# Macaron stage: order of VectorE's work in a step, form of five small VectorE operations, and where GpSimd adds and scales

## The reference

```python
def attn_layer(x, Wqkv, qs, ksc, Wo):              # x is shift_tokens(x), 16 heads of 64
    q, k, v = split(x @ Wqkv)
    q = l2norm(q) * qs;  k = l2norm(k) * ksc       # one length per token and head
    q = q * cos * scale + rotate_half(q) * sin * scale
    k = k * cos * inv + rotate_half(k) * sin * inv
    ...                                            # windows of 32: this one and the one before, softmax, times v
    return out @ Wo
def ffn_layer(x, g, bln, W1, b1, W2, b2):          # x is shift_tokens(x)
    xn = (x - mean) / sqrt(var + 1e-05) * g + bln
    a, gate = split(xn @ W1 + b1)
    return a * gelu(gate) @ W2 + b2
```

## Time and profile before

| | |
|---|---|
| median of 3 runs | 4523.4 us (4511.47 to 4524.17) |
| the profiled execution | 4541.07 us, span 4539.3 us |
| busy share of the span | PE 89%, VectorE 74%, GpSimd 60%, ScalarE 58% |
| macaron stages | 50 to about 1847 us and 1942 to about 3741 us of the span, with the linear attention between them |
| chain that ended last | PE 66%, VectorE 17%, issue 8%, ScalarE 4%, GpSimd 4% |

### The profile page before, as it was taken

One profiled execution on the slowest core, in us unless ns is written; L12 is line 12 of the kernel. 1 busy time (PEld: TensorE's weight loads), 2 busy tenths in 40 slices (PEclk: granted clock), 3 DMA queues, 4 the chain that ended last, 5 costly groups with the idle time before them and its releaser, 6 DMA issues.

```text
span 4539.3 us, 161990 instructions
## 1 busy us (share of the span) xinstructions
PE 4035.5 (89%) x70897; PEld 2573.9 (57%) x70897; DVE 3337.3 (74%) x5613; ACT 2635.8 (58%) x4548; POOL 2704.3 (60%) x3554
## 2 busy tenths in 40 slices
PE   4999999999999999479999999999999985899975
PEld 2666666666666666346666666666666653333333
DVE  5887788878877877478778888788777754667744
ACT  3666666666666665046666666666666641356651
POOL 4777777777777776277777777777777760100000
PEclk9999999999999999789999999999999997689996
DMA  2000000000000000000000000000000000000000
GB/s 81 5 4 24 9 8 20 9 23 7 7 23 9 23 5 9 20 3 9 4 24 10 24 4 9 23 10 23 4 9 5 5 4 0 1 1 1 1 1 9
DMA packets 75299, 53.51 MB, mean 12 GB/s; under 512 B 48472, under 2 KB 71400, under 8 KB 72944
## 3 DMA queue, kind: packets, MB, share of 16 engines
q1 hardware_dynamic: 74608, 43.28, 3.4%
HBM read 35.93 MB, written 1.05 MB: 8 GB/s over the span
## 4 chain that ended last, share of the span: by engine, by line
PE 66%; DVE 17%; issue 8%; ACT 4%; POOL 4%; DVEq 1%; SPq 0%; POOLq 0%; DMA 0%; ACTq 0%
PE psum L343 8%; PE psum L354 8%; PE psum L365 7%; PE psum L427 7%; DVE turn L631 6%; PE psum L390 5%; PE psum L408 5%; PE psum L419 3%; DVE den L676 3%; PE psum L1148 3%; PE psum L490 3%; PE psum L507 3%; PE psum L1117 2%; PE psum L497 2%; PE psum L1136 2%
## 5 line engine op out<-in xcount | busy, mean ns | idle before, releaser
L631 DVE TENSOR_TENSOR turn<-psum,ropes 128x512 f32<-128x512 f32 x1536 | 937.4, 671 | 23.7 <-POOL qkr L734 19.0
L741 POOL TENSOR_TENSOR turn<-turn 128x1024 f32<-128x1024 f32 x384 | 904.1, 2377 | 7.9 <-DVE turn L631 7.9
L343 PE MATMUL psum<-wqkv,xT 128*128 128x512 f32 x1536 | 769.0, 624 | 43.4 <-DVE turn L631 41.2
L526 ACT ACTIVATE sq<-psum 128x512 f32<-128x512 f32 x768 | 456.0, 594 | 578.0 <-PE psum L343 577.9
L734 POOL TENSOR_TENSOR qkr<-turn,rn 128x1024 f32<-128x1024 f32 x384 | 753.3, 1983 | 15.1
L768 POOL TENSOR_TENSOR scratch<-scratch,rden 128x1024 f32<-128x1024 f32 x192 | 365.7, 1905 | 658.0 <-DVE rden L679 658.0
L408 PEld LDWEIGHTS psum<-scratch,V 32*64 32x64 f32 x29952 | 547.3, 132 | 182.7 <-issue 181.4
L408 PE MATMUL psum<-scratch,V 32*64 32x64 f32 (+1 forms) x29952 | 592.7, 222 | 6.7 <-issue 4.6
L354 PE MATMUL psum<-wqkv,xT 128*64 128x512 f32 x1536 | 435.1, 646 | 124.1 <-DVE turn L631 124.1
L365 PEld LDWEIGHTS psum<-ident,qkr 128*128 128x128 f32 x3072 | 340.7, 145 | 353.4 <-ACT kT L535 154.3
L365 PE MATMUL psum<-ident,qkr 128*128 128x128 f32 x3072 | 479.8, 291 | 11.8 <-POOL qkr L734 11.8
(11 more groups left out here) (181 smaller groups left out, 6362.7 us busy)
## 6 DMA issues: line engine op xcount, KB each, us to landing
wqkv<-in_L_ffn_Wqkv_dram SPq DMA_DIRECT2D x12, 1536.0 KB, 7.2
wo<-in_L_ffn_Wo_dram SPq DMA_DIRECT2D x12, 512.0 KB, 7.5
zs<-Y SPq DMA_DIRECT2D x192, 31.8 KB
w<-in_L_ffn_W_dram SPq DMA_DIRECT2D x12, 341.0 KB
zs<-Y SPq DMA_DIRECT2D x168, 0.2 KB
w<-in_L_ffn_W_dram SPq DMA_DIRECT2D x12, 128.0 KB
rope<-in_shape_consts_dram SPq DMA_DIRECT2D x1, 1024.0 KB
X<-in_L_attn_x_dram SPq DMA_DIRECT2D x2, 512.0 KB
```

The source lines that it names most:

```text
L343: pe.matmul(bank[b][:, :], xT[:, n // TPB % 2, bass.ts(n % TPB, P)], wqkv[n // TILES % 2][:, INNER * w:INNER * w + INNER].rearrange("p (h ...
L526: act.activation(sq[:, q // 2, q % 2, :, :], bank[QK_BANK[q]][:, :].rearrange("p (h d) -> p h d", d=RH), ACT.Square).then_inc(sem("squared ...
L631: e = dve.tensor_tensor(dst, src, tab.unsqueeze(1).broadcast_to([P, HEADS, RH]), ALU.mult)
L741: pool.tensor_tensor(t1, t1, turn2[:, w, :, :, :].rearrange("p a h d -> p (a h d)"), ALU.add).then_inc(sem("added"), 1)
```

## The change

Five things move or change form.

VectorE's order in a step: `rotate(u, 0)` and `rotate(u, 1)` follow the subtraction of the maximum, ahead of the softmax sum; the statistics of v and the norm of z come after `rotate(u, 3)`; the aggregation of the statistics stands between the two `lengths`. The two norm operations become `scalar_tensor_tensor` with the inverse root broadcast from `rn` as a tensor in SBUF; the addition of epsilon and the floor become `tensor_tensor` with constant tiles `eps` and `least` in SBUF. GpSimd's `add` writes its sum into `qkr`, in the order that the transposes read, and for that waits until the last transposes of the tile before have read `qkr`; `scale` multiplies `qkr` in place. `rotate(u, 0)` and `rotate(u, 2)` wait for the `add` of the tile before, where they waited for its `scale`. The shifted tile `zs` has three buffers where it had two. The attention over V used two PSUM banks before as after; the diff has nothing on it.

```diff
-        zs = sb("zs", [P, 2, HALF])
+        zs = sb("zs", [P, 3, HALF])
+        least = sb("least", [P, 32])
...
-            if n >= 2:
-                sp.wait_ge(sem("unit_normed"), at.part(n - 2, "unit_normed"))
+            if n >= 3:
+                sp.wait_ge(sem("unit_normed"), at.part(n - 3, "unit_normed"))
...
                 if on(n - 1) and a == 0:
-                    dve.wait_ge(sem("qk_rotated"), part(n - 1, "qk_rotated", w))
+                    dve.wait_ge(sem("added"), part(n - 1, "added", w))
...
-                if on(z):
-                    dve.wait_ge(sem("rnorm"), at.step(s - 1))
-                    if on(z - 1):
-                        dve.wait_ge(sem("mixed"), mixed(s - 1))
-                    dve.tensor_scalar(zn[:, 0:HALF], Y[:, z % TILES, 0:HALF], mv[:, 0:1], rn[:, 32:33], ALU.subtract,
-                                      ALU.mult)
-                    dve.tensor_scalar(zn[:, HALF:D], zs[:, z % 2, :], mv[:, 0:1], rn[:, 32:33], ALU.subtract,
-                                      ALU.mult).then_inc(sem("unit_normed"), 1)
-                if on(v):
-                    dve.wait_ge(sem("shifted%d" % (v % 2)), at.shifted(v))
-                    dve.bn_stats(st6[:, 0, :], Y[:, v % TILES, 0:HALF])
-                    dve.bn_stats(st6[:, 1, :], zs[:, v % 2, :]).then_inc(sem("unit_stats"), 1)
                 if on(u):
                     rotate(u, 0)
-                if on(v):
...
-                    dve.bn_aggr(mv[:, :], st6[:, :, :]).then_inc(sem("unit_moments"), 1)
+                    rotate(u, 1)
                 if on(t):
                     dve.wait_ge(sem("exp_done"), part(t, "exp_done"))
...
                 if on(u):
-                    rotate(u, 1)
                     rotate(u, 2)
                     rotate(u, 3)
+                if on(v):
+                    dve.wait_ge(sem("shifted%d" % (v % 3)), at.shifted(v))
+                    dve.bn_stats(st6[:, 0, :], Y[:, v % TILES, 0:HALF])
+                    dve.bn_stats(st6[:, 1, :], zs[:, v % 3, :]).then_inc(sem("unit_stats"), 1)
                 if s > FIRST_STEP:
                     dve.wait_ge(sem("rnorm"), at.step(s - 1))
+                if on(z):
+                    if on(z - 1):
+                        dve.wait_ge(sem("mixed"), mixed(s - 1))
+                    inv = rn[:, 32:33].broadcast_to([P, HALF])
+                    dve.scalar_tensor_tensor(zn[:, 0:HALF], Y[:, z % TILES, 0:HALF], mv[:, 0:1], inv, ALU.subtract,
+                                             ALU.mult)
+                    dve.scalar_tensor_tensor(zn[:, HALF:D], zs[:, z % 3, :], mv[:, 0:1], inv, ALU.subtract,
+                                             ALU.mult).then_inc(sem("unit_normed"), 1)
+                if on(u):
+                    lengths(u, 0)
+                if on(v):
...
+                    dve.bn_aggr(mv[:, :], st6[:, :, :]).then_inc(sem("unit_moments"), 1)
+                if on(u):
+                    lengths(u, 1)
                 if on(v):
                     dve.wait_ge(sem("unit_moments"), part(v, "unit_moments"))
-                    dve.tensor_scalar(ss[:, 32:33], mv[:, 1:2], LN_EPS, None, ALU.add).then_inc(sem("unit_var"), 1)
+                    dve.tensor_tensor(ss[:, 32:33], mv[:, 1:2], eps[:, 0:1], ALU.add).then_inc(sem("unit_var"), 1)
                 if on(u):
-                    lengths(u, 0)
-                    lengths(u, 1)
                     dve.wait_ge(sem("summed"), part(u, "summed", 1))
-                    dve.tensor_scalar(ss[:, 0:32], ss[:, 0:32], 1e-24, None, ALU.max).then_inc(sem("norms_squared"), 1)
+                    dve.tensor_tensor(ss[:, 0:32], ss[:, 0:32], least[:, :], ALU.max).then_inc(sem("norms_squared"), 1)
...
             def scale(n, w):
-                r = rn[:, 16 * w:16 * w + 16]
+                rows = qkr[:, w, :].rearrange("p (h d) -> p h d", d=DH)
                 pool.wait_ge(sem("added"), part(n, "added", w))
+                pool.tensor_tensor(rows, rows, bc(rn[:, 16 * w:16 * w + 16], DH), ALU.mult).then_inc(
+                    sem("qk_rotated"), 1)
+
+            def add(n, w):
+                pool.wait_ge(sem("turned"), part(n, "turned", 2 * w + 1))
                 if on(n - 1):
                     pool.wait_ge(sem("qk_turned"), part(n - 1, "qk_turned", 2 * w + 1))
                 pool.tensor_tensor(qkr[:, w, :].rearrange("p (h a d) -> p a h d", a=2, d=RH), turn1[:, w, :, :, :],
-                                   r.unsqueeze(1).unsqueeze(3).broadcast_to([P, 2, HEADS, RH]),
-                                   ALU.mult).then_inc(sem("qk_rotated"), 1)
-
-            def add(n, w):
-                pool.wait_ge(sem("turned"), part(n, "turned", 2 * w + 1))
-                t1 = turn1[:, w, :, :, :].rearrange("p a h d -> p (a h d)")
-                pool.tensor_tensor(t1, t1, turn2[:, w, :, :, :].rearrange("p a h d -> p (a h d)"), ALU.add).then_inc(
-                    sem("added"), 1)
+                                   turn2[:, w, :, :, :], ALU.add).then_inc(sem("added"), 1)
```

More of the change, by code:

```diff
@@ L87, in shifted @@
     def shifted(self, n):
-        return 32 * (self.macaron * NT // 2 + n // 2 + 1)
+        return 32 * (self.macaron * NT // 3 + n // 3 + 1)
     def masked(self, n):
@@ L268, in shift_tile @@
         def shift_tile(sp, at, n):
-            y, z = Y[:, n % TILES, HALF:D], zs[:, n % 2, :]
+            y, z = Y[:, n % TILES, HALF:D], zs[:, n % 3, :]
             sp.wait_ge(sem("attn_added"), at.part(n, "attn_added"))
-            if n >= 2:
-                sp.wait_ge(sem("unit_normed"), at.part(n - 2, "unit_normed"))
-            sp.dma_start(z[1:P, :], y[0:P - 1, :]).then_inc(sem("shifted%d" % (n % 2)), 16)
+            if n >= 3:
+                sp.wait_ge(sem("unit_normed"), at.part(n - 3, "unit_normed"))
+            sp.dma_start(z[1:P, :], y[0:P - 1, :]).then_inc(sem("shifted%d" % (n % 3)), 16)
             row = zero_row if n % TPB == 0 else Y[P - 1:P, n % TILES - 1, HALF:D]
-            sp.dma_start(z[0:1, :], row).then_inc(sem("shifted%d" % (n % 2)), 16)
+            sp.dma_start(z[0:1, :], row).then_inc(sem("shifted%d" % (n % 3)), 16)
         zero_row = const[1:2, 384 + 4 * TPB * DH:384 + 4 * TPB * DH + HALF]
@@ L680, in step @@
                 if on(u):
-                    rotate(u, 1)
                     rotate(u, 2)
                     rotate(u, 3)
+                if on(v):
+                    dve.wait_ge(sem("shifted%d" % (v % 3)), at.shifted(v))
+                    dve.bn_stats(st6[:, 0, :], Y[:, v % TILES, 0:HALF])
+                    dve.bn_stats(st6[:, 1, :], zs[:, v % 3, :]).then_inc(sem("unit_stats"), 1)
                 if s > FIRST_STEP:
                     dve.wait_ge(sem("rnorm"), at.step(s - 1))
+                if on(z):
[9 more added lines that the diff above has]
+                if on(v):
+                    dve.wait_ge(sem("unit_stats"), part(v, "unit_stats"))
+                    if on(z):
+                        dve.wait_ge(sem("unit_normed"), part(z, "unit_normed"))
+                    dve.bn_aggr(mv[:, :], st6[:, :, :]).then_inc(sem("unit_moments"), 1)
+                if on(u):
+                    lengths(u, 1)
                 if on(v):
                     dve.wait_ge(sem("unit_moments"), part(v, "unit_moments"))
-                    dve.tensor_scalar(ss[:, 32:33], mv[:, 1:2], LN_EPS, None, ALU.add).then_inc(sem("unit_var"), 1)
+                    dve.tensor_tensor(ss[:, 32:33], mv[:, 1:2], eps[:, 0:1], ALU.add).then_inc(sem("unit_var"), 1)
                 if on(u):
-                    lengths(u, 0)
-                    lengths(u, 1)
                     dve.wait_ge(sem("summed"), part(u, "summed", 1))
-                    dve.tensor_scalar(ss[:, 0:32], ss[:, 0:32], 1e-24, None, ALU.max).then_inc(sem("norms_squared"), 1)
+                    dve.tensor_tensor(ss[:, 0:32], ss[:, 0:32], least[:, :], ALU.max).then_inc(sem("norms_squared"), 1)
                     dve.wait_ge(sem("norms_squared"), part(u, "norms_squared"))
@@ L1396, in _ @@
             dve.memset(eps[:, :], LN_EPS)
+            dve.memset(least[:, :], 1e-24)
             dve.memset(ones[:, :], 1.0)
```

3 lines of the change are left out of this document (removed).

## The result

After the change the kernel takes 4771.4 us, median of 4 runs (4755.22 to 4795.58); the kernel before, beside it, 4523.78 (4511.47 to 4524.78). The ratio is 1.0558, with a 95% interval of 1.0499 to 1.0618: slower, by more than the prediction's range allowed. The profiled execution took 4795.58 us with a span of 4793.8; the mean granted clock fell from 0.951 to 0.912.

The account below looks back on a forecast made before the run. A ring of 18.57 us per step was to bound the kernel: +52 us for two stages and +33 for clock falls, +85 of 4541, on the median 4608 us. Range 4370 to 4650; the first case's own 4560 to 4660.

Parts of the forecast that it names:

- the ring: Per step, transposes, adds, norm, sums, Newton, scale and transposes again take 18.57 us, so all steps take that time.
- 64.6: A stage's first four steps have no norm; their ring is 16.1 us each, 64.6 us together.
- the port: VectorE's two norm operations, asked for during GpSimd's first add, wait for both adds: about 1.9 and 2.4 us.
- The third rival: Norm operations with two SBUF inputs don't wait mid-flight, only hold GpSimd up: ring 16.0 us, kernel 4377 us; chance 0.22.
- the second rival: Both norm operations pass at 12.98, with no add between them: ring 16.7 us, kernel 4412 us; chance 0.25.
- the first case: Both norm operations wait, one for each add: ring 18.57 us, kernel 4608 us; chance 0.45.
- the clock: Gate steps: clock falls in half of 22 a stage, 1.5 us each, +33 for both stages; in all +66.
- The rope-scaling steps: Counted like ordinary steps, among 90 a stage at 18.57 us, 1671.3 us together, with nothing added.
- 85: Total loss in us: +52 for two stages from the ring, +33 from clock falls; 1.9% of 4541.
- the fourth: GpSimd's strided add takes 3.3 us or more instead of 2.36: the ring grows by 1.9 us; chance 0.03.
- The fifth: The change makes no difference, the ring landing between 18.1 and 18.3 us; chance 0.05.
- the prediction's own bound: If the norm delays the first guess of the inverse roots by less than about 2.1 us, the kernel gets faster.

Follow-up runs that it names:

- experiment 1: The changed kernel with the two norm operations as tensor_scalar again, at their new place: 4757.04 us, ratio 1.0488 to the kernel before.
- experiment 2: The changed kernel without the two norm operations, a small memset signalling in their place: 4398.33 us, ratio 0.9702 to the kernel before.
- experiment 3: The changed kernel with the two norm operations moved between the softmax sum and its inverse: 4397.64 us, ratio 0.9708 to the kernel before.
- experiment 5: The changed kernel with three unused projections added on PE in each gate step, ahead of the waiting transposes: 4681.65 us, ratio 1.0311 to the kernel before.
- experiment 8: The changed kernel with the old adds and scales, and the norm between softmax sum and its inverse: 4394.73 us, ratio 0.9692 to the kernel before.
- experiment 9: The kernel of experiment 3 with PE's first transposes of the scaled q behind the attention's second half: 4371.69 us, ratio 0.963 to the kernel before.

## Why the prediction was off: the mechanism held, two terms of the sum did not

**Right: the ring.** The prediction had the pair wait for both adds, 1.9 and 2.4 us; the medians are 2.05 and 2.39. It had four steps at 4 x 18.57 = 74.3, the trace has 73.95 where the clock holds. It had the wait for the scale at 2.9 us in gate steps, it is 2.75; it had the floor at 0.2, it is 0.19; `zn` 0.3 late, it was 0.16; and PE waits for a rotation at only two places, for 4.7 us. In the second macaron the 81 regular steps without the falls took 1497.7 us (21 plain 334.9, 22 gate at 21.11, 22 up 398.8, 16 out 299.5), where 81 x 18.57 is 1504.2. What did not hold is that each step takes the ring's time, with steps of 18.5 to 18.9 as the sign of it: counted from PE's scores they take 15.9, 21.1, 18.3 and 18.6, since PE meets the ring's whole excess at one place, in the gate step. The first eight took 139.2, and the prediction's 64.6 + 4 x 18.57 is 138.9; this agreement is in part luck, as three of the eight have a fall of the clock, which that sum has not.

**Right: the port.** Experiments 1, 2 and 3 show that mid-flight arrival decides: 0.28 us at one place, 2.0 and 2.4 at the other, in either form. The third rival, that an operation with two SBUF inputs does not wait there, is refuted. The rule of the Trainium skill ("SBUF — State Buffer", section "Who interferes with whom"), by which the instruction that comes second waits out the first, agrees for the first of the pair: it ended with the add in flight. That the second lost its turn as well to the next add was read from L661 in the earlier trace rows, and it decided the second rival, which would have been faster. The prediction wrote down the first case's 4608 to that rule, but the first norm operation waits until 12.98 in the second rival too; what parts the two is the second operation alone.

**Wrong, and by most: the clock.** The step that failed is "A fall costs 1.5; in half of 22 gate steps a stage it is +33 for both". The falls came in 42 of 44 gate steps, and one costs 2.75 us (23.86 against 21.11; 2.9 in the mean of the 42). Over both stages the regular gate steps took 520.6 + 531.0 = 1051.6 us where 44 x 21.11 is 928.8: +122.8, not +33, and not the +66 that the range's end allowed. The 1.5 came from a step in which PE had waited about 2 us in two pieces; here it idles 2.75 in one, and in the step shown 7.0 us at 0.51 follow. The falls of before had been rarer and mostly shorter, and I took their number and size over to a longer idle piece. Experiment 5 confirms the term: with the idle piece filled the clock stays up, and the 44 gate steps take 928.6 us.

**Wrong: the rope-scaling steps.** "After: 90 steps at 18.57 are 1671.3" takes for ordinary ones the steps in which VectorE also scales the tables (L616), five in a stage. In the second macaron they took 22.3 us on average before and take 24.3 now, 121.5 for five, against 92.9 in the sum: +57.4 for both stages. The two instructions show why:

```profile
649.93 2.75 DVE L616 TENSOR_TENSOR ropes<-rope,qks 128x256 f32<-128x256 f32 x8
649.95 2.82 POOL L755 TENSOR_SCALAR rt<-rt 128x33 f32<-128x33 f32 x1
...
656.00:664.00 8.00, 7.46 (x93) 4.52 (x94) 5.11 (x9) 3.31 (x7) 4.16 (x3) 0.57 0.01 2
```

L616 holds one of GpSimd's Newton operations, usually 0.22 us, for 2.82. In a ring that sets the time this is added whole: PE waits 2.65 us ahead of the transposes, and the clock falls to 0.57 (the last row, a window). The 5.7 us by which such a step exceeds 18.57 are thus, as an estimate, 2.6 of L616 and one fall of 2.9, so that half of the 57 is the clock once more. Where the ring has slack, in experiment 3, a rope-scaling step takes 18.74 us, 0.7 more than another out step, and no fall comes. Before the change it took 4.2 more (22.3 against 18.05), with falls in seven of ten. The rows for L616 were at hand; the sum did not use them where the ring was the bound.

Together: 90 more for the gate steps' clock, 57 for the rope-scaling steps, 6 less elsewhere in these steps, 3 because the sum took the second macaron's 1710.0 for the first too (1707.0), and 26 outside these steps. That makes the 170 by which 254.5 exceeds 85. The 26 can't be put down to the change: outside these steps the traces took from 1112 to 1169 us, whatever the kernel (1122 before, 1148 after, 1120 in experiment 3, 1159 in experiment 8). They took longer the more time PE spent there at the lower clock, from 348 us in experiment 3 to 479 in experiment 5.

**The other rivals.** The strided add is not dearer (2366 ns in the mean, as estimated), so the fourth falls. The fifth, no change, falls too. By the prediction's own bound, a norm that delays the guess less than 2.1 us makes the change faster: with no delay it gives the 0.97 of experiment 3.

**Left open.** Rotations wait 331.7 us in all for ScalarE's square. This helps to set when the norm is asked for: in the up step rotation 3 waited 0.52 us for it, and the pair came 0.39 after the add had begun. Whether an earlier fourth square would let the pair pass ahead of the adds was not tried. In experiment 9 four steps take 69.1 us (15.31, 17.89, 17.89 and 17.99) with PE busy 68.8, so in regular steps next to nothing is left to gain from waits.

## What to carry to other kernels

Before moving a small VectorE operation, look at what GpSimd runs at the new time, not at how long the operation took at the old one: 0.27 us became 2.4, twice in a row, because two long GpSimd operations stood there. When a wait on TensorE becomes one long piece instead of several short ones, price the clock behind it by a row with a piece as long, and in every step that has it; and when a ring becomes the bound, add every stall on it, those of rare steps too. If such a change comes out slower, move the one operation before giving up the rest: here that alone turned 5.6% slower into 2.9% faster, and later transposes on PE made it 3.7%.

## What the runs showed of the hardware beside that

A VectorE operation on one int32 input of 33 columns, L704, the first guess of the inverse roots, also waits for a GpSimd add in flight. In the gate step at 452.45 the pair ran before the adds and was free (0.28), and the guess waited instead. VectorE, then GpSimd:

```profile
468.37 0.27 DVE L678 SCALAR_TENSOR_TENSOR zn<-Y,mv,rn 128x64 f32<-128x64 f32 x1
468.56 0.28 DVE L680 SCALAR_TENSOR_TENSOR zn<-zs,mv,rn 128x64 f32<-128x64 f32 x1
...
471.56 2.23 DVE L704 TENSOR_SCALAR rn<-ss 128x33 int32<-128x33 int32 x1
```

```profile
469.04 4.71 POOL L742 TENSOR_TENSOR qkr<-turn 128x1024 f32<-128x1024 f32 x2 [4.50 <-PE psum L366]
```

L704 ends at 473.79 and the second add at 473.75. In the same stretch the sums of squares L637 (one input of 1024 columns) ran beside the adds in 1.21 and 1.17 us, their usual length.

At the places shown, the turn goes to the operation that starts first. Eight adjacent L616, the first of them started 0.02 us ahead of GpSimd's L755 (649.93 against 649.95), kept it out for all of their 2.75 us. The two adjacent norm operations of the up step let GpSimd's second add in between, and that add had started 0.05 us ahead of the second of them (489.36):

```profile
489.31 2.35 POOL L742 TENSOR_TENSOR qkr<-turn 128x1024 f32<-128x1024 f32 x1
```

No run moved these starts against each other, so it is not shown that their order decides.
